# Recommender tower on one core: GpSimd's gathers get a small write behind each and other waits for TensorE, and one pad fill moves

## What is computed

```python
e = stack([tbl_f[ids[:, f]] for f in range(26)], axis=1)        # 512 x 26 x 128
all_emb = concatenate([bottom_output[:, None, :], e], axis=1)   # 512 x 27 x 128
gram = einsum('bfd,bgd->bfg', all_emb, all_emb)
z = gram[:, _TRIU_I, _TRIU_J]                                   # 512 x 351
h = concatenate([z, bottom_output], axis=1)
h = maximum(h @ W_top1 + b_top1, 0.0)                           # 479 -> 512
h = maximum(h @ W_top2 + b_top2, 0.0)                           # 512 -> 256
y = h @ W_top3
```

## Time and profile before

| | us |
|---|---|
| time before, median of 3 runs | 126.42 |
| lowest and highest of them | 126.39 and 127.14 |
| the profiled execution, its own time | 126.88 |
| its span, first to last instruction | 125.1 |
| TensorE matmuls busy in it | 105.8 |
| GpSimd busy in it | 70.6 |

### The profile page before, as it was taken

How to read it: one execution, slowest core, us unless ns; L and a number is a source line. 1 busy time by engine, 2 the same in 40 slices (tenths; PEclk the granted TensorE clock), 3 DMA queues, 4 the chain that set the end, 5 groups by cost and what they waited for, 6 DMA issues and landing times.

```text
span 125.1 us, 1970 instructions
## 1 busy us (share of the span) xinstructions
PE 105.8 (85%) x702; PEld 93.6 (75%) x702; DVE 62.4 (50%) x148; ACT 53.2 (43%) x97; POOL 70.6 (56%) x77
## 2 busy tenths in 40 slices
PE   0599999994999999989941998799579399999993
PEld 0277888883865888779941998699569299999891
DVE  3489999975699999217403020512033122641220
ACT  4555785147598453345404261502212282532111
POOL 2788787788588858775783668573847300017000
PEclk9999999999999999999999599999999999999999
DMA  3897959831799910121120222132212101002000
GB/s 80 288 242 204 242 166 258 235 77 46 208 244 347 242 42 24 47 63 42 42 60 24 76 70 70 30 82 52 73 26 60 42 0 43 24 1 63 0 0 1
DMA packets 7481, 12.31 MB, mean 98 GB/s; under 512 B 3420, under 2 KB 4356, under 8 KB 7472
## 3 DMA queue, kind: packets, MB, share of 16 engines
q1 hardware_dynamic: 5200, 7.78, 22.7%
q0 software_dynamic: 2208, 4.36, 13.6%
q10 hardware_dynamic: 64, 0.07, 0.2%
HBM read 11.40 MB, written 0.00 MB: 91 GB/s over the span
## 4 chain that ended last, share of the span: by engine, by line
PE 64%; ACT 10%; another core or an unknown queue 8%; issue 6%; SPq 4%; DMA 4%; ACTq 1%; DVE 1%
PE psX L396 15%; PE psG L438 14%; PE psX L397 14%; PE psL L468 7%; PE psL L483 4%; SPq L285 4%; ACT featT L534 4%; PE psL L458 3%; PE psL L492 2%; PE psX L411 2%; ACT hi L544 2%; DMA feat<-in_tbl,idx 2%; DMA zT<-z 2%; ACT z L557 2%
## 5 line engine op out<-in xcount | busy, mean ns | idle before, releaser
L350 POOL DMA_INDIRECT feat<-in_tbl,idx x64 | 67.2, 1049 | 29.5 <-issue 17.2
L396 PE MATMUL psX<-onehot,hi 125*128 125x512 f32 x82 | 33.9, 413 | 2.0 <-ACT hi L544 1.7
L438 PE MATMUL psG<-featT 128*123 128x108 f32 x256 | 31.0, 280 | 4.8 <-ACT z L557 4.4
L438 PEld LDWEIGHTS psG<-featT 128*123 128x123 f32 x256 | 30.0, 196 | 5.4 <-ACT z L557 4.5
L397 PE MATMUL psX<-onehot,lo 125*128 125x512 f32 x82 | 33.0, 403 | 0.0
L628 DVE TENSOR_SCALAR onehot<-ids_rel 125x512 fp32r<-125x512 f32 x82 | 29.7, 429 | 1.8 <-issue 1.4
L638 DVE COPY z<-psG 27x216 f32<-27x216 f32 x32 | 12.2, 383 | 23.2 <-PE psG L438 13.9
L534 ACT ACTIVATE featT<-psX 128x512 f32<-128x512 f32 (+2 forms) x21 | 17.1, 828 | 13.5 <-PE psX L397 10.6
L396 PEld LDWEIGHTS psX<-onehot,hi 125*128 125x128 f32 x82 | 16.1, 196 | 7.2 <-issue 3.2
L557 ACT ACTIVATE z<-psG 27x216 f32<-27x216 f32 x32 | 10.9, 340 | 23.8 <-PE psG L438 13.5
L397 PEld LDWEIGHTS psX<-onehot,lo 125*128 125x128 f32 x82 | 16.1, 197 | 3.2
(11 more groups left out here) (30 smaller groups left out, 53.9 us busy)
## 6 DMA issues: line engine op xcount, KB each, us to landing
whole<-in_tbl SPq DMA_DIRECT2D x8, 448.0 KB
feat<-in_tbl,idx POOLq DMA_INDIRECT x64, 2.5
w1z<-in_w_pairs SPq DMA_DIRECT2D x1, 768.0 KB
whole<-in_tbl SPq DMA_DIRECT2D x1, 560.0 KB
w<-in_W SPq DMA_DIRECT2D x1, 512.0 KB
whole<-in_tbl SPq DMA_DIRECT2D x2, 224.0 KB
whole<-in_tbl SPq DMA_DIRECT2D x8, 52.0 KB
bottomT<-in_bottom_t SPq DMA_DIRECT2D x1, 256.0 KB
```

Source lines behind the costliest of these rows:

```text
L350: nc.gpsimd.indirect_dma_start(feat[:, k % FU, i, :], None, tables[f - 1], bass.IndirectOffsetOnAxis(idx[:, t, f - 1:f], 0)).then_inc(rows ...
L396: nc.tensor.matmul(out, hi[:, q % PB, r, :], onehot[:, c % RV, :], start=(r == 0), stop=False)
L438: done = nc.tensor.matmul(psG[n % 2][0:FS * (GS - 1) + F, g // GB, (g % GB) * GS * F:(g % GB + 1) * GS * F], later, four[:, :, 0:F], start ...
```

## The change

Three things are edited.

1. Behind each of the 28 gathers of units 9 to 16 GpSimd fills one column (128x1, fp32) of a new tensor `unread` with zeros. Nothing reads it, nothing waits for it and it increments no semaphore.
2. `WATCH` goes from 17 to 24 entries, and may now name lookups (o76: `onehot_used` at 77 or more) and transposes (t8: `units_transposed` at 9 or more). Most of the entries that stay stand one gather earlier (g3 from 10.3 to 10.2, g4 from 11.1 to 11.0, a1 from 13.0 to 12.3, a4 from 16.0 to 15.2); g0, g1, g2 and a0 go.
3. VectorE's fill q0 moves behind the last one-hot.

```diff
+    PACED = 9
     WATCH = {tuple(int(n) for n in w.split(":")[0].split(".")): (w.split(":")[1][0], int(w.split(":")[1][1:]))
-             for w in """9.2:g0 10.0:g1 10.1:g2 10.3:g3 11.1:g4 11.2:g5 12.0:g6 12.2:g7 12.3:a0 13.0:a1 13.1:a2 13.2:a3
-        13.3:g8 14.2:g9 14.3:b1 15.2:g10 16.0:a4""".split()}
+             for w in """8.1:o76 8.2:o79 8.3:o81 9.1:t6 9.3:t7 10.1:t8 10.2:g3 11.0:g4 11.1:g5 11.2:t9 11.3:g6 12.0:t10
+        12.1:g7 12.3:a1 13.0:a2 13.1:a3 13.3:g8 14.0:t12 14.1:g9 14.2:b0 14.3:b1 15.0:t13 15.1:g10 15.2:a4""".split()}
-    DVE_PLAN = steps("""l0 o2 l1 o8 l2 o11 l3 l4 o9 l5 o14 q0 l6 l7 o8 l8 o5 l9 o16 l10 o9 z0 q1 z1 q2 z2 q3 z3 z4 z5 a0 z6
+    DVE_PLAN = steps("""l0 o2 l1 o8 l2 o11 l3 l4 o9 l5 o14 l6 l7 o8 l8 o5 l9 o16 l10 o9 q0 z0 q1 z1 q2 z2 q3 z3 z4 z5 a0 z6
+        unread = sb("unread", [P, len(units) - PACED, TU])
-                        pool.wait_ge({"g": gram_done, "a": l1_done, "b": l2_done}[kind], n + 1)
+                        pool.wait_ge({"o": onehot_used, "t": units_transposed, "g": gram_done, "a": l1_done, "b": l2_done}[kind], n + 1)
                     nc.gpsimd.indirect_dma_start(
                         feat[:, k % FU, i, :], None, tables[f - 1],
                         bass.IndirectOffsetOnAxis(idx[:, t, f - 1:f], 0)).then_inc(rows_in[k], 16)
+                    if k >= PACED:
+                        nc.gpsimd.memset(unread[:, k - PACED, i:i + 1], 0.0)
```

## The result

| | before | changed | changed to before, 95% interval |
|---|---|---|---|
| the first chip, median us of 21 runs each | 127.09 | 126.58 | 0.9945 (0.9918 to 0.9972) |
| a later chip, median us of 23 and 12 runs | 116.63 | 116.84 | 1.0021 (0.9988 to 1.0053) |

On the first chip the change brings 0.55%, 0.7 us, where 3.4 were forecast; on another it brings nothing, and there both kernels are 10 us faster. The ratios leave out executions over 1.5% above the fastest of their kernel (on the first chip 7 of the 21 changed ones), and with all of them but one of 211.07 us the two means are 127.1 and 127.1, so even the 0.7 us are not certain.

What follows compares the result with a forecast made beforehand. TensorE's late reports were taken as the bound, GpSimd's queue close behind. Gain 5.4 - 2.0 = 3.4 us: 126.88 - 3.4 = 123.5, less 0.46 for the profiled execution standing above the median, 123.0; range 119.5 to 129.0.

Steps and rivals of the forecast that it cites:

- While gathers follow each other, a report of TensorE can be held up, and a pause lets it through: Gathers of units 9 to 16: late reports cost TensorE 9.4 + 1.6 = 11.0 us at most.
- Its benefit can only be that reports of TensorE get through. If all do ...: Small writes between gathers: with all reports in time, t16 can use its rows from 96.6, ending 5.4 us sooner.
- a third of the pauses: GpSimd's pauses for TensorE's reports between gathers: of 5.9 us, 2.0 stay, chosen between none and all.
- 27 x 0.10 = 2.7 us: GpSimd's queue, gathers 9.0 to 16.0: each write adds its own duration of 0.10 us, hidden only by the pauses.
- The waits: New WATCH entries: bind nowhere with punctual reports; otherwise g3's report comes 1.25 us sooner, counted in the 2.0 us.
- With all reports in time GpSimd's queue sets the pace: Middle part: gathers 1.35 us apart, TensorE waits 1.3 to 1.8 us before t10 to t13, end 5.4 us sooner.
- The pad fill q0: VectorE, moved behind the last one-hot: ends over 2 us before needed; gives at most 0.59 us, taken as 0.
- the change touches next to nothing in the lookup part: Lookup part, before the middle part: next to nothing touched there; the question is when t16 can run.
- the second: GpSimd's queue: write does nothing either way, waits only shift pauses, 126 to 127 us, no change; chance 0.15.

Runs made afterwards that it cites:

- e1: The kernel before with only the 28 small writes added, old waits and q0 at its old place: 132.12 us median beside 131.79 on a late chip.
- e4: The changed kernel with GpSimd's wait for g3 moved from 10.2 to 10.0 and entry 10.1:t8 dropped, late chip: ratio 1.0016 to the kernel before.
- f1: The changed kernel as it is, timed beside the kernel before on a punctual chip: ratio 1.0021, middle part 39.0 us.
- g2: The changed kernel with four instead of three buffers of gathered rows, late chip: ratio 0.9914 (0.9689 to 1.0139) to the kernel before.
- k1: The changed kernel with the 28 gathers of units 9 to 16 replaced by plain DMAs of 128 consecutive rows, late chip: ratio 0.9098 to the kernel before.

## Why the prediction was wrong, step by step

**"While gathers follow each other, a report of TensorE can be held up, and a pause lets it through": right, on some chips.** Taking the late gathers away gives back 11.3 us where 11.0 were worked out (9.4 of waits and 1.6 of slow clock), though about 2.3 of them are waits for gathered rows that late reports don't explain. Leaving all waits out makes g3 8.1 us late. What the trace of one execution could not show is that the lateness changes from chip to chip: on three of the six later ones g3 is read within 0.2 us.

**"Its benefit can only be that reports of TensorE get through. If all do ...": the step that failed.** Nothing in the trace showed a write letting a report through. I made it the likeliest case and let a third of the pauses stay. All stayed: 5.9 became 6.6. With the writes alone (e1) g3's report is 5.3 us late, as before. By the runs the write is neutral, in its benefit and in its price. What passed for evidence, that the write is another kind of work than a gather, was none; the trace had already shown that a gap of 0.30 often doesn't help, and the write only fills that gap.

**"27 x 0.10 = 2.7 us": too high by all of it.** The spacing stays 1.25, so the write costs 0. The row that I took, its own duration of 0.10, was the wrong kind of row. The Trainium skill (Perfetto Trace Analysis, GPSIMD Engine Instruction) told to go by the spacing of starts; the runs agree with that and not with my choice. With a free write and 2.0 us of pauses my sum would have been 120.3, still further off, so this error hid a part of the other.

**The waits: right in mechanism, and what they give is given back.** I wrote that one gather earlier brings g3's report 1.25 sooner. It came 1.4 sooner (3.9 late instead of 5.3). But the half clock stayed, and the wait for gathered rows grew from 1.3 to 2.1. e4 shows the trade at its full size: TensorE's wait behind g3 is 0.9 us instead of 4.4, and those for gathered rows are 4.7 instead of 1.3.

**"With all reports in time GpSimd's queue sets the pace": right in kind, too large in size.** On a punctual chip GpSimd issues all 28 gathers at 1.25, and t16 starts 2.6 us after the last of them (91.84 and 89.22 in f1). But TensorE waits for gathered rows twice, 0.6 and 0.8 us, where I had four waits of 1.3 to 1.8 with a distance of 1.35. The 0.10 too much makes 0.4 over four gathers of a unit. The first g also starts 0.9 us later against gather 9.0 than my numbers had it (2.7 us before it in f1, 3.5 in the kernel before).

**The pad fill q0: right, as far as seen.** It ran from 54.65 to 55.24, after the last one-hot and before g0 at 57.80, with the same 0.47 us between lookup and g0. No run has this edit alone. At its old place nothing can be read off either, because of the next point.

**What I took for quiet.** I wrote that the change touches next to nothing in the lookup part. On late chips this part holds most of the spread: the first g starts at 53.5 to 60.8 us in the ten profiles. The first row is the kernel before, the second the changed one:

```profile
31.01 0.47 PE L396 MATMUL psX<-onehot,hi 125*128 125x512 f32 x1 [1.70 <-ACT hi L544]
```

```profile
33.70 0.77 PE L401 MATMUL psX<-onehot,hi 125*128 125x512 f32 x1 [3.86 <-DVE lo L625]
```

That stall of TensorE was 1.0 to 6.6 us in nine of the ten profiles from late chips (the tenth, g2, has one of 4.1 us at 42 instead), and absent in all profiles from punctual ones. It goes with the late reports (ScalarE waits for lookups' reports before it makes the next high halves), and the change doesn't touch it. That it has the same cause is likely and not shown, since no run changed it alone on a late chip.

Of the rivals, the second, given 0.15, is what happened: the write does nothing in either direction and the waits only shift the pauses, 126 to 127. It had one step wrong too: it hid 2.7 us of writes in 2.1 us of slack, which doesn't fit, and the runs needed no hiding.

## What to carry to other kernels

When an engine's work has ended and several readers start late at the same moment, the delay is in the report. Look at what runs then, and take that away in one experiment before you build a cure on a guess of what lets reports through. Where two bounds lie close together (here late reports and GpSimd's queue), a pause that cures one is paid from the other, so count both before moving waits. And time such a kernel on several chips: what one profile shows as its largest loss may be missing on the next.

## What the hardware showed that I had not expected

- The same kernel takes 116.6 to 117.0 us on three chips, 129.1 to 131.8 on three others and 127.1 on the first. The difference lies in how late TensorE's reports reach the other engines while gathers follow each other (at g3 0.2 us or up to 8.1). The mean granted clock of the kernel before is 1.000 on punctual chips in all executions but one, and 0.93 to 0.99 on the late ones. It follows from the gaps: with plain DMAs it is 1.000 on a late chip too (k1).
- Of the three kinds of work tried in GpSimd's queue only the indirect DMAs came with late reports. 1,000-column writes back to back (11.35 us) and plain DMAs of the same size (in series of at most 2.75 us) left g3's report punctual on a late chip, in one profile each.
- The Trainium skill (SBUF — State Buffer, Who interferes with whom) says that a DMA never contends with a compute engine. TensorE's matmuls indeed run at their usual pace beside the gathers (5.31 us for 48 without, 3.59 for 32 with them, 0.11 each), but what other engines learn of them comes late. The page's rule is one of memory ports and speaks of no reports, so for those the measurement stands alone.
- A 128x1 write behind a gather costs GpSimd nothing: 0.95 + 0.11 + 0.19 is again 1.25.
